# Weight units spread anew over attention's first blocks and feed-forward's first slots, x's transposes behind the key step, softmax exponentials first on ScalarE

## The reference, cut to what matters

```python
x = _layernorm(x + _L0_attn_ref(x, ...))         # 8 heads of 8, softmax, output projection
x = _layernorm(x + _L0_xattn_ref(ctx, ctx, x))   # softmax(ctx x^T) over the rows of each batch
x = _layernorm(x + _L0_ffn_ref(x, ...))          # x W^T + b + one of four low-rank updates, chosen per row
x = _layernorm(x + _L1_attn_ref(x, ...))         # (q+k+v)/3 by NF4 weights, projection, gated FFN by NF4 weights
x = _layernorm(x + _L1_xattn_ref(x, ctx, ...))   # cross attention on ctx
x = _layernorm(x + _L1_ffn_ref(x, ...))          # silu(x G^T) * (x U^T), then down; ternary weights
```

## Time and profile before

| | us |
|---|---|
| median of 3 runs | 650.83 |
| lowest and highest of them | 650.7 and 651.41 |
| the profiled execution, whole | 652.39 |
| its span in the trace | 650.5 |
| TensorE busy in the span | 634.7 (98%) |
| VectorE busy | 396.3 (61%) |
| ScalarE busy | 382.9 (59%) |
| GpSimd busy | 70.6 (11%) |
| mean granted TensorE clock | 0.992 of full speed |

### The profile page before, as it was taken

How to read it: one execution, slowest core, us unless ns; L and a number is a source line. 1 busy time by engine, 2 the same in 40 slices (tenths; PEclk the granted TensorE clock), 3 DMA queues, 4 the chain that set the end, 5 groups by cost and what they waited for, 6 DMA issues and landing times.

```text
span 650.5 us, 8517 instructions
## 1 busy us (share of the span) xinstructions
PE 634.7 (98%) x3224; PEld 470.6 (72%) x3224; DVE 396.3 (61%) x633; ACT 382.9 (59%) x527; POOL 70.6 (11%) x116
## 2 busy tenths in 40 slices
PE   8999999999989999999999999999999999999996
PEld 6555545544547888888888888887777888888874
DVE  4878787667886967776857447324764221215567
ACT  2977799966886597757677145223465433326522
POOL 1132142312350000000000000001221000000012
PEclk9999999999979999999999999999999999999998
DMA  7871585504242333323330003048000322100002
GB/s 249 294 240 36 168 269 185 161 12 130 65 141 79 96 105 108 108 73 105 108 104 1 2 0 131 1 150 335 1 33 2 85 93 76 54 1 0 1 32 98
DMA packets 25590, 63.92 MB, mean 98 GB/s; under 512 B 5541, under 2 KB 10725, under 8 KB 24782
## 3 DMA queue, kind: packets, MB, share of 16 engines
q1 hardware_dynamic: 23294, 61.68, 29.3%
q10 hardware_dynamic: 2256, 1.70, 0.9%
HBM read 58.77 MB, written 4.60 MB: 97 GB/s over the span
## 4 chain that ended last, share of the span: by engine, by line
PE 87%; DVE 5%; ACT 5%; issue 2%; POOL 1%; POOLq 0%; DVEq 0%; ACTq 0%
PE bank L1047 18%; PE bank L1035 8%; PE bank L1034 8%; PE bank L1036 8%; PE bank L1125 8%; PE bank L1126 8%; PE bank L886 4%; PE bank L802 3%; PE bank L606 3%; PE bank L741 2%; PE bank L1101 1%; PE bank L916 1%; PE bank L718 1%; PE bank L930 1%; PE bank L988 1%
## 5 line engine op out<-in xcount | busy, mean ns | idle before, releaser
L1236 ACT ACTIVATE line<-line 128x1024 f32<-128x1024 f32 x87 | 91.3, 1049 | 0.2
L1035 PE MATMUL bank<-xl,wh 128*128 128x512 f32 x224 | 87.4, 390 | 0.0
L1034 PE MATMUL bank<-xh,wh 128*128 128x512 f32 x224 | 87.4, 390 | 0.0
L1036 PE MATMUL bank<-xh,wl 128*128 128x512 f32 x224 | 87.3, 390 | 0.0
L1047 PE MATMUL bank<-wh,xh 128*128 128x512 f32 x192 | 76.0, 396 | 0.2 <-DVE xl L2127 0.2
L1047 PE MATMUL bank<-wh,xl 128*128 128x512 f32 x192 | 74.8, 390 | 0.0
L2210 DVE SCALAR_TENSOR_TENSOR arena<-bank,ff_s,arena 128x512 f32<-128x512 f32 x28 | 21.0, 751 | 72.9 <-PE bank L1126 63.4
L2127 DVE TENSOR_TENSOR xl<-arena,xh 128x1024 fp32r<-128x1024 f32 (+1 forms) x26 | 29.7, 1141 | 35.4 <-ACT xh L1543 35.3
L1125 PE MATMUL bank<-xh,wh 128*128 128x512 f32 x128 | 50.2, 392 | 0.0
L1126 PE MATMUL bank<-xl,wh 128*128 128x512 f32 x128 | 49.9, 390 | 0.0
L1543 ACT ACTIVATE xh<-arena 128x1024 fp32r<-128x1024 f32 (+1 forms) x26 | 25.6, 991 | 41.3 <-PE bank L1047 34.8
(11 more groups left out here) (219 smaller groups left out, 1268.2 us busy)
## 6 DMA issues: line engine op xcount, KB each, us to landing
codes<-in_c_gu SPq DMA_DIRECT2D x14, 512.0 KB, 3.6
scales<-in_s_gu SPq DMA_DIRECT2D x28, 256.0 KB, 3.9
codes<-in_t_gu SPq DMA_DIRECT2D x8, 512.0 KB, 3.7
codes<-in_c_dn SPq DMA_DIRECT2D x7, 512.0 KB, 4.8
scales<-in_s_dn SPq DMA_DIRECT2D x14, 256.0 KB, 4.0
fold<-in_t_dn SPq DMA_DIRECT2D x1, 3584.0 KB, 15.5
codes<-in_c_qkv SPq DMA_DIRECT2D x6, 512.0 KB, 4.5
scales<-in_t_gu SPq DMA_DIRECT2D x6, 512.0 KB, 3.8
```

The costliest lines, as they stand in the source:

```text
L1034: pe.matmul(dst, wh[:, s, c:c + P], xh[:, k, cols], start=(k == 0), stop=False)
L1035: pe.matmul(dst, wh[:, s, c:c + P], xl[:, k, cols], start=False, stop=False)
L1036: last = pe.matmul(dst, wl[:, s, c:c + P], xh[:, k, cols], start=False, stop=(k == KD - 1))
L1236: nc.scalar.activation(below(slot), below(slot), ACT.Prelu, bias=bias, scale=scale, alpha=alpha).then_inc(bent, 1)
```

## The change

Four edits. The second `warm_up`, ahead of `place_heads`, issues two products instead of one. In attention's slots 2 to 6, `x_T` moves on TensorE from ahead of `scores_T` (slot 2: from ahead of the key step) to behind the key step that follows `scores_T`, and on ScalarE `x_T_out` moves from ahead of `heads_exp` to behind it. VectorE's units in attention's slots 1 to 4 are spread anew. And feed-forward's slots take 2, 1, 1, 2, 2, 2, 1, 1 units instead of 1, 2, 1, 1, 2, 2, 2, 1. No instruction is removed, and none is added but the one product of the `warm_up`, which the trace shows as two passes.

```diff
--- before.py
+++ after.py
@@ -94,7 +94,7 @@
 WARM = 4
 
 
-PLAN = ([0] + [1] * (NT - 1), [2], [0, 1, 1, 1, 2] + [1] * 4, [1, 2, 1, 1, 2, 2, 2, 1, 0, 0])
+PLAN = ([0] + [1] * (NT - 1), [2], [0, 1, 1, 1, 2] + [1] * 4, [2, 1, 1, 2, 2, 2, 1, 1, 0, 0])
 PLAN_END = [sum(map(sum, PLAN[:n + 1])) for n in range(len(PLAN))]
 assert PLAN_END[1] < 2 * C_DN and PLAN_END[2] <= 2 * C_DN + NF - 6 and PLAN_END[-1] == U_GU
 
@@ -812,7 +812,7 @@
 
             warm_up(WARM)
             qk_projection(0)
-            warm_up(1)
+            warm_up(2)
             place_heads()
             qk_projection(1)
             scores(0)
@@ -834,19 +834,15 @@
                     v_rows(1)
                     key_step(0)
                 o_proj(t - 1)
-                if 2 < t < NT - 1:
-                    x_T(0, t - 2)
                 scores_T(t)
                 if t == 1:
                     qk_projection(3)
-                elif t == 2:
-                    x_T(0, 0)
-                    key_step(1)
                 elif t == NT - 1:
                     key_biases(KD + 1)
+                for n in steps[1:2]:
+                    key_step(n)
+                if t > 1:
                     x_T(0, t - 2)
-                for n in steps[1:2] if t > 2 else ():
-                    key_step(n)
                 if t + 1 < NT:
                     scores(t + 1)
                 heads_out(t)
@@ -1353,11 +1349,8 @@
                 if t == NT - 1:
                     key_group_out(KD)
                 unit_bends(t - 1, 0)
-                if t < NT - 1:
-                    x_T_out(t - 2)
                 heads_exp(t)
-                if t == NT - 1:
-                    x_T_out(t - 2)
+                x_T_out(t - 2)
                 if t > 2:
                     key_group_out(t - 3 if t < NT - 1 else KD + 1)
                 unit_bends(t - 1, 1)
@@ -1908,14 +1901,22 @@
                 augment(t)
                 if t == 1:
                     unit_part(0, 0)
+                elif t == 2:
+                    unit_part(0, 1)
+                elif t == 3:
+                    unit_part(1, 1)
+                    unit_part(2, 0)
+                elif t == 4:
+                    unit_part(3, 0)
+                    unit_part(3, 1)
                 else:
-                    if t == 2:
-                        unit_part(1, 0)
                     unit_part(t - 1, 1)
                 attention_norm(t - 1)
-                if t == 1:
-                    unit_part(0, 1)
-                else:
+                if t == 2:
+                    unit_part(1, 0)
+                elif t == 3:
+                    unit_part(2, 1)
+                elif t > 3:
                     unit_part(t, 0)
                 if t + 1 < NT:
                     row_max(t + 1)
```

## The result

| | before | after |
|---|---|---|
| median, us | 650.83 (650.7 to 652.21, 6 runs) | 645.26 (644.71 to 646.33, 6 runs) |
| ratio, 95% interval | | 0.9911 (0.9898 to 0.9924) |
| the profiled execution, whole | 652.39 | 645.23 |
| its span | 650.5 | 643.1 |
| mean granted clock | 0.992 | 0.998 |

The change makes the kernel 5.6 us faster by these medians, 5.8 by the ratio. The kernel after was run twice more, beside other executions of before: 645.42 against 651.40 (e13) and 645.34 against 651.63 (e17), 6.0 and 6.3 us. The forecast was a gain of 8.6 us and a time of 642.2, with a range up to 645.0; the result lies 0.3 us above the range. Lines of the kernel after are 4 lower than before for TensorE's from L833 on and for ScalarE's up to L1324, 7 lower for ScalarE's L1447 and L1457 and for VectorE's and GpSimd's.

What follows compares the result with a forecast made beforehand. TensorE was taken to bound the kernel, its waits all in the first third. Attention 2.3, ffn_W's wait 0.7 and the lmT wait with its clock fall 5.6 sum to 8.6: 650.83 to 642.2 us, range 641.0 to 645.0.

Steps and rivals of the forecast that it cites:

- start of place_heads: Second warm-up ahead of place_heads: its added product was taken to cost 0, at most 0.5 us.
- slots 1 and 2: Attention: row_max(2) 0.6 us earlier, and scores(3) 1.2 us earlier with that included, ScalarE's bend being late next.
- slots 3 to 6: Attention: o_proj to scores takes 3.07 us instead of 3.35, 0.28 less in each of four slots, 1.1 us.
- to slot 6's lora_out: Feed-forward: ffn_W(5) no longer waits for VectorE's sum, 0.7 us, and TensorE's wait for lmT goes, 2.2 us.
- The difference of the runs should be that of the spans: Last step: the forecast gain of 8.6 us taken straight off the median, 650.83 - 8.6 = 642.2.
- the 3.4 us: TensorE's loss at 1.2 GHz behind the lmT wait in the profiled execution of before, counted as won.
- the same chain one slot on: Feed-forward, late next: m_high(3) to attention_out; VectorE ends it at about 187.0, TensorE comes at 187.5.
- the tightest codes: Among SyncE's loads, codes for feed-forward's slot 6 land 0.3 us ahead of their bend, whose norm has 1.4 us slack.
- The rival that attention gives nothing: VectorE's maxima set attention's ring; slots 3 to 6 give 0, slots 1 and 2 only 0.6: 643.9; chance 0.12.
- The slack of 0.3 us between the four bends and the norm: Feed-forward: the four bends end at 177.5, 0.3 us ahead of the norm's new time of 177.8.
- the slower rival: Bends in feed-forward's slots 4 and 5 wait for scaled, giving two pauses with clock falls: 653.4; chance 0.05.
- The pause moves: Rival: TensorE pauses 1.5 us near attention_out instead and the clock still falls: 647.1; chance 0.09.

Runs made afterwards that it cites:

- e13: The kernel after, unchanged, run again beside other executions of before: 645.42 us, ratio 0.9907.
- e17: The kernel after, unchanged, a third time, beside the version that loads chunk 1's codes earlier: 645.34 us, ratio 0.9906.
- e14: The kernel before, unchanged, profiled a third time: 651.31 us, one execution.
- e1: The kernel before, unchanged, for more executions and a second trace: 651.89 us, ratio 1.0008.
- e15: The kernel before, unchanged, profiled a fourth time: 653.13 us, one execution.
- e5: The kernel before with five products nobody reads filling TensorE's pause ahead of slot 6's lora_out: 651.21 us, ratio 0.9997.
- e10: The kernel after with a pause put back: slot 6's lora_out waits for ScalarE's second bend of that slot: 646.60 us, ratio 0.9928.

## Why the prediction was wrong

The order of things was right and the sum too large. By the profiled executions of before and after:

| term | forecast | measured |
|---|---|---|
| start of place_heads | 0 | -0.67 (7.53, 8.20) |
| slots 1 and 2 | 1.2 | 0.97 (25.54, 24.57) |
| slots 3 to 6 | 1.1 | 0.99 (30.45, 29.46) |
| to slot 6's lora_out | 0.7 + 2.2 | 3.05 (122.15, 119.10) |
| behind it | 3.4 | 3.09 (38.02, 34.93) |
| sum | 8.6 | 7.43 (span 7.4) |

By their whole times these two executions are 7.16 us apart (652.39, 645.23), and 1.56 of that is how far the profiled before stood above its own median: that leaves 5.6.

**The step that failed** is the last one, "The difference of the runs should be that of the spans", together with the 3.4 us that it carried over. The profiled execution of before was 1.56 us above its median, 652.39 against 650.83, and I knew both numbers. The 3.4 us were read correctly from its rows, but, by the mean clocks, a fall of that size belongs to 8 of 72 executions. In the others the piece behind the pause takes 36.0 to 36.4 us, and the change takes it to 34.93: it wins 1.0 to 1.4 us there and not 3.4. With 1.4 for 3.4, and 651.6 as before's time, the measured terms give 651.6 - 0.97 - 0.99 - 3.05 - 1.4 = 645.2. The 650.83 that the forecast started from was 0.8 us under the median of the 72, by the chance of few runs; from it the same terms give 644.4, within the range. A rival with this term at half its size would have had to stand beside the forecast; I had none. The gap between the profiled time and the median was the sign of it.

**A second step failed beside it**: a slower clock was counted in full. While TensorE runs at half speed the other engines go on, and whatever waits for them behind it covers a part. I looked for what is late next in the kernel after ("the same chain one slot on") and not in the kernel before, where that chain is already late enough for a wait of 0.86 us once the clock is up (e14).

**Slots 1 and 2**: the 1.2 us was right in mechanism, with ScalarE's bend late next; how it splits between units and order hangs on the codes, as shown above. `row_max(2)` starts 17.85 us behind `place_heads` (26.05 - 8.20), which in the first trace's time is 25.38, where 25.4 was forecast. What I left out is a load: I took L1228 to start without a wait since it did so in the one trace, and said that the tightest codes are those of feed-forward's slot 6, 0.3 us early. Those landed 0.53 us late in after's trace and cost nothing; the codes of attention's slot 2 cost 0.4 us there (24.57 against 24.13), up to 0.9 in other traces.

**Slots 3 to 6**: 0.25 us each for 0.28. TensorE's piece is 3.10 us for the 3.07 forecast, without a wait. The rival that attention gives nothing is refuted.

**Feed-forward**: right to 0.2 us. `ffn_W(5)` has no wait. The prediction's times there leave out what attention wins, if the 2.3 in its 185.67 - 2.3 - 0.7 (182.67, there 182.6) is the pause, as the rest fits; it does not say so. In after's trace `scores(7)` is 1.3 us earlier than before; with that taken off, `lora_T_out(6)` was forecast at 180.1 and is at 180.28, `lora_out(6)` at 181.3 and is at 181.33. GpSimd's step took 0.57 us in its new place, against 1.59 in the earlier trace rows with a join beside it. This agrees with the page SBUF — State Buffer of the Trainium skill (Who interferes with whom), by which a VectorE instruction with two SBUF inputs contends with a GpSimd instruction that reads SBUF. The slack of 0.3 us between the four bends and the norm is gone: the last of them ends at 176.52, the norm starts at 176.56. No row of ScalarE in slots 4 and 5 has a wait on the joins or the scaling, so the slower rival fell. New is a wait of 0.2 us for `xl`, which no forecast had:

```profile
182.54 0.63 PE L606 MATMUL bank<-ident,x 128*128 128x128 f32 x4 [0.19 <-DVE xl L1810]
```

**The pause moves**: it doesn't. And its price would have been less than the rival said: a pause of 1.4 us put back at `lora_out(6)` costs 1.2 us.

## What to carry to other kernels

Before a price is read from a profiled execution, see how far its own time stands from the median; where it is off by as much as a term of the sum, the largest term that may differ between executions (a clock, a load's landing) is to be sized down, or given a rival of its own. A stretch at the lower clock cost here TensorE's loss less what the other engines would have made it wait anyway, so look for that wait in the kernel before. And where an edit brings a chain forward, check each load that this chain meets against the time at which it lands, also where the old trace shows no wait for it.

## What the runs showed of the hardware

Behind the same pause of 2.15 us, in the same program, the granted clock once stayed at 1.00 (e14), and in other executions TensorE lost 1.7 us (e1) or 3.4 us (e15 and the first trace) at 1.2 GHz. With the pause filled it stayed up in the trace, and no execution of 11 had the lower means (e5). A pause of 1.4 us had no fall behind it in its trace (e10). I had expected the fall to belong to the pause, and it belongs to the execution as much. Why it differs stays open; no run here tells it.
